# Swapping the order of the recurrent product's blocks between even and odd steps

## The reference

```python
h = silu(cond @ W1.T + b1)
gate = sigmoid(h @ W2.T + b2)
x = x + (x + x * gate)        # x * (2 + gate)
```

```python
def step(prev_h, xw):                   # xw = x[:, t] @ Wx + b
    next_h = tanh(prev_h @ Wh + xw)
    return next_h, next_h
x = x + h_t
```

## Time and profile before

| what | us |
|---|---|
| median of 3 runs (197.01 to 197.09) | 197.02 |
| the profiled execution | 196.62 |
| its span, first to last instruction | 194.8 |
| TensorE matmuls busy | 176.0 |
| TensorE weight loads busy | 167.4 |
| VectorE busy | 98.2 |
| ScalarE busy | 85.3 |

### The profile page before, as it was taken

How to read it: one execution, slowest core, us unless ns; L and a number is a source line. 1 busy time by engine, 2 the same in 40 slices (tenths; PEclk the granted TensorE clock), 3 DMA queues, 4 the chain that set the end, 5 groups by cost and what they waited for, 6 DMA issues and landing times.

```text
span 194.8 us, 33383 instructions
## 1 busy us (share of the span) xinstructions
PE 176.0 (90%) x15962; PEld 167.4 (86%) x15962; DVE 98.2 (50%) x395; ACT 85.3 (44%) x518; POOL 0.5 (0%) x5
## 2 busy tenths in 40 slices
PE   4899999999999999999999999999999999999995
PEld 2698988988898898889889889888988988898895
DVE  0445465455546545555554654555465455545543
ACT  3234444444444444444444444444444444444442
POOL 1000000000000000000000000000000000000000
PEclk9999999999999999999999999999999999999999
DMA  6309999702020020202002020200202020020212
GB/s 200 109 30 320 397 415 406 294 1 108 0 107 3 0 109 0 108 0 107 1 2 108 0 109 0 106 2 2 108 0 108 0 100 9 0 109 0 108 54 54
DMA packets 7105, 17.98 MB, mean 92 GB/s; under 512 B 1459, under 2 KB 2867, under 8 KB 7094
## 3 DMA queue, kind: packets, MB, share of 16 engines
q1 hardware_dynamic: 6656, 17.32, 23.8%
q10 hardware_dynamic: 438, 0.55, 0.8%
HBM read 9.48 MB, written 8.39 MB: 92 GB/s over the span
## 4 chain that ended last, share of the span: by engine, by line
PE 86%; ACT 7%; issue 3%; DMA 3%; SPq 0%
PE bank_e L193 48%; PE bank_l L193 38%; ACT h_ring L178 7%; DMA w_t<-in_w 3%; SPq L129 0%
## 5 line engine op out<-in xcount | busy, mean ns | idle before, releaser
L193 PE MATMUL bank_e<-h_ring,wh_sb 128*32 128x32 f32 x4096 | 98.6, 204 | 13.5 <-ACT h_ring L178 13.5
L178 ACT ACTIVATE h_ring<-bank_e 128x32 f32<-128x32 f32 x256 | 50.5, 197 | 101.7 <-PE bank_e L193 101.7
L193 PE MATMUL bank_l<-h_ring,wh_sb 128*32 128x32 f32 x4096 | 91.2, 196 | 0.0
L193 PEld LDWEIGHTS bank_e<-h_ring,wh_sb 128*32 128x32 f32 x4096 | 71.5, 108 | 20.2 <-ACT h_ring L178 20.1
L193 PE MATMUL bank_l<-x_ring,wx_sb 128*32 128x32 f32 (+1 forms) x4112 | 81.0, 200 | 0.0
L341 DVE TENSOR_TENSOR x<-x,h_ring 128x128 f32<-128x128 f32 x129 | 37.6, 291 | 84.0 <-ACT h_ring L178 84.0
L193 PE MATMUL bank_e<-x_ring,wx_sb 128*32 128x64 f32 (+1 forms) x2056 | 71.0, 224 | 0.0
L193 PEld LDWEIGHTS bank_l<-h_ring,wh_sb 128*32 128x32 f32 x4096 | 69.8, 113 | 0.0
L193 PEld LDWEIGHTS bank_l<-x_ring,wx_sb 128*32 128x32 f32 (+1 forms) x4112 | 64.5, 111 | 0.0
L193 PE MATMUL bank_l<-ones,b_sb 128*32 128x32 bf16 (+1 forms) x1026 | 51.7, 180 | 0.0
L178 ACT ACTIVATE h_ring<-bank_l 128x32 f32<-128x32 f32 x256 | 50.4, 197 | 0.0
(11 more groups left out here) (31 smaller groups left out, 14.0 us busy)
## 6 DMA issues: line engine op xcount, KB each, us to landing
x<-in_x SPq DMA_DIRECT2D x15, 512.0 KB, 9.5
out_dram<-x SPq DMA_DIRECT2D x15, 512.0 KB, 3.5
w_t<-in_w SPq DMA_DIRECT2D x1, 256.0 KB, 5.4
wx_sb<-in_wx SPq DMA_DIRECT2D x1, 256.0 KB, 5.7
wh_sb<-in_wh ACTq DMA_DIRECT2D x1, 256.0 KB, 5.0
x<-in_x SPq DMA_DIRECT2D x1, 256.0 KB, 3.1
out_dram<-x SPq DMA_DIRECT2D x1, 256.0 KB, 2.5
w_t<-in_w_cond ACTq DMA_DIRECT2D x1, 145.0 KB, 3.8
```

The source lines that it names most:

```text
L178: nc.scalar.activation(h_ring[:, m, s * B:(s + 1) * B], z_of(s, m), ACT.Tanh)\
L193: done = nc.tensor.matmul(out[q:q + columns], weights[:, q:q + columns], moving, start=start, stop=stop, skip_group_check=True)
```

## The change

The condition in the list of orders is turned round. Steps 0 and 2 of a turn now make (0, 0), (1, 0), (0, 1), (1, 1), in which half one of z is whole after two blocks; steps 1 and 3 now make (0, 0), (0, 1), (1, 0), (1, 1), in which it is whole after three. The fills, the waits for each half of h and the number of matmuls are the same.

```diff
-                    order = [(0, 0), (1, 0), (0, 1), (1, 1)] if s % 2 else [(0, 0), (0, 1), (1, 0), (1, 1)]
+                    order = [(0, 0), (1, 0), (0, 1), (1, 1)] if s % 2 == 0 else [(0, 0), (0, 1), (1, 0), (1, 1)]
```

## The result

The changed kernel takes 199.26 us (median of 5 runs, 198.83 to 199.62) against 197.01 us before: 1.014 times as long (95% interval 1.012 to 1.017). In a second comparison the same pair came out at 1.017 (1.014 to 1.020), so 3 us is the better figure for the difference. The profiled execution is 199.59 us, 2.97 more than the one before.

What follows compares the result with a forecast made beforehand. The kernel was taken as bound by a loop of latencies, not TensorE's throughput. Late fills add 0.02 x 64 + 0.06 x 63 = 5.1 us to 197.0; with a little regained at the loop's head, 202.0 us, range 200.0 to 205.2.

Steps and rivals of the forecast that it cites:

- The loop of gap + 0.59: Every step, tanh to tanh: a closed loop of latencies, the two tanhs' gap + 0.25 + 0.34 us.
- the exchange of the gaps: Between ScalarE's two tanhs: 0.16 moves to steps 1 and 3, 0.09 to 0 and 2; the turn's sum stays 0.50.
- A: Order (0,0), (1,0), (0,1), (1,1): gap 0.16; the fill after it starts 0.12 us ahead of the tanh, not 0.19.
- the engine was not full: Rival in TensorE: its throughput sets the end, so the time stays 197.0 us; chance 0.06.
- the gap did not jump: Rival at ScalarE's second tanh: gap grows by 0.07 behind late steps, 206.6 us, or 211 if twice a turn; chance 0.08.
- B: Order (0,0), (0,1), (1,0), (1,1): gap 0.09; now in steps 1 and 3, whose fills were to end late.
- Step 1: Its fill ends at +0.32 instead of +0.25, half one's second product 0.03 late: cost 0.02 us a turn, 64 times.
- my low bound: Counting only weight loads: step 1 costs 0.01 or less, step 3 0.045; 0.05 a turn, 3.2 us.
- Step 3: Its fill ends at +0.36, half one's second product 0.065 late: cost 0.055 to 0.06 us a turn, 63 times.
- The loop's head: Rival at step 0's first products: waits in every fourth turn vanish, 0.6 us gained, 196.4 us; chance 0.04.
- the main case: Late fills in steps 1 and 3 make it slower, 200.2 to 205.2 us; chance 0.82.

Runs made afterwards that it cites:

- the shorter fill: Changed kernel with the wide block moved to step 2's fill and 4 bias records moved from step 1's to step 3's fill: 1.001 of the kernel before.
- the extra block: Changed kernel with one block of 8 records added to step 3's fill: 1.051 of the kernel before; same addition in the kernel before: 1.032.
- all B: Changed kernel with the order (0,0), (0,1), (1,0), (1,1) in all four steps: 1.008 of the kernel before.
- the split kernel: Changed kernel with block (0,1) split in two, half before and half after block (1,0), in all steps: 1.017 of the kernel before.

## Why the prediction was too high

**The mechanism held.** The loop of gap + 0.59, the exchange of the gaps, the fills that start 0.07 closer to their tanh behind A, the place of the loss (steps 1 and 3, not 0 and 2) and the order of the two costs all came as written. The wide block moved from step 3's to step 2's fill (2.860) takes step 3's loss away, the shorter fill takes step 1's away, and the extra block adds its whole length. The rivals fell: the engine was not full, and the gap did not jump: it stayed 0.09 behind the late B steps.

**Step 1: 0.02 forecast, 0.017 measured** (0.761 against 0.744). That this agrees is in part luck. TensorE's matmuls in this step, of which the rows are the first of half one's second product and its last:

```profile
98.44 0.21 PE L193 MATMUL bank_e<-h_ring,wh_sb 128*32 128x32 f32 x1
...
98.54 0.20 PE L193 MATMUL bank_e<-h_ring,wh_sb 128*32 128x32 f32 x1
```

The second product started 0.42 after the tanh at 98.02, not 0.45. Its records then took 0.10 where I had 0.065, and the tanh at 98.78 followed the last one by 0.24 instead of 0.26. These errors nearly cancel. The loads alone, my low bound, have it right: 0.42 against 0.41.

**Step 3: 0.06 forecast, 0.041 measured.** This is the step that failed: "I take the middle because the trace shows matmuls 0.03 behind their loads in a full stream". The loads' own reckoning, which I had set down as the low bound, gave the second product of half one at +0.46 against 0.41 and a cost of 0.045; it was loaded at +0.45. Half one's last matmul was indeed recorded as late as I had added up, 0.55 after the tanh (0.48 and 0.065), but the next tanh followed it sooner:

```profile
99.99 0.20 PE L193 MATMUL bank_e<-h_ring,wh_sb 128*32 128x32 f32 x1
100.00 0.20 PE L193 MATMUL bank_l<-h_ring,wh_sb 128*32 128x32 f32 x1
100.00 0.20 PE L193 MATMUL bank_e<-h_ring,wh_sb 128*32 128x32 f32 x1
100.02 0.25 PE L193 MATMUL bank_l<-h_ring,wh_sb 128*32 128x32 f32 x6
```

The last record on bank_e starts at 100.00 and the tanh at 100.24: 0.24. In the kernel before, the last of the eight records from 96.44 starts near 96.51 (their row lasts 0.27, one matmul 0.20), and the tanh comes at 96.77: 0.26. My reading is that after a wait the records start in a burst, while in a full stream they are spread out and stand nearer to the work itself; all B, below, bears it out. From the first load of half one's second product to the tanh it is 0.34 in both. A distance from a recorded matmul start in a waiting step must not be added to a start in a full stream. The Trainium skill has a line that fits (Perfetto Trace Analysis, Summary: the profiler window per engine type): for TensorE the start is that of the operands' prefetch and the end is estimated. The trace agrees in so far as a recorded start is no fixed time ahead of the tanh: 0.24 and 0.26 above.

**The loop's head: up to 0.6 us forecast as a rival's gain, of which I counted 0.1; it came whole.** The stall of every fourth turn made the kernel before 2.851 a turn instead of 2.843. In the changed kernel no steady turn shows it, neither in the tanhs nor in step 0's first load, which comes 0.25 after its tanh in every one: the mean of 2.901 is the sum of the four steps. The 0.008 a turn are 0.5 us. It is no rival to the main case but a term of its own sum, since both rest on TensorE's place against the tanh, and it had a row of its own. The store, which I gave as its cause, is not it (stores moved half a turn, above).

**The sum, then:** 0.017 x 64 + 0.041 x 63 - 0.5 = 3.2 us, where the mean turns give 3.1, the two comparisons 2.8 (1.014) and 3.3 (1.017), and I had 5.0. Of the 1.9 us between 5.0 and the turns' 3.1, step 3 makes 1.2, step 1 0.2 and the loop's head 0.4 beyond the 0.1 counted. The low bound took the two costs nearly right (0.05 a turn, 3.2 us) but only 0.2 off for the loop's head; with the 0.5 it gives 199.7, still above the 199.26 measured. That last part, the 0.8 us between the turns' 3.1 and the 2.3 of the medians, no run explains.

**What my later expectations got wrong.** B behind B was put at 0.705 and is 0.72. Two blocks take 0.12 in recorded loads after a wait (96.13 to 96.25) but 0.13 in a full stream, and the first number is a burst. That error of 0.013 in all four steps turned a forecast gain of 2 us into a loss of 1.5. All B itself shows it, for its step 3 runs in a full stream and lasts 0.72 all the same (tanhs at 98.04 and 98.76). Half one's second product is loaded there at

```profile
98.42 0.11 PEld L193 LDWEIGHTS bank_e<-h_ring,wh_sb 128*32 128x32 f32 x1
```

which is 0.38 after the one tanh and 0.34 ahead of the other, where the steps that wait have 0.36 and 0.35. So the recorded starts shift and the work does not. It is the same mistake as in step 3.

## What to carry to other kernels

When a loop of latencies is the bound, reckon each piece of filler work by when it may start and when it has to end: the order of the blocks that depend on the loop can be neutral for the loop and still shift that window, here by 0.07 us. Before swapping such an order, look which steps carry the longest filler and put the order with the early finish behind them, or move filler to a step with cover; here the same change then cost nothing that could be measured (1.001). Measure distances for such sums between events of the same kind in the same state, both after a wait or both in a full stream, and take an idle stretch for free room only when its idle time is a wait for data, not "issue".

## What the runs showed of the hardware

- Going round TensorE's loop takes 0.37 to 0.42 us from the last weight load of a turn to the next load, even where that waits for nothing (97.93 to 98.33), with 0.045 more in every second, third or fourth turn or in none, depending on the kernel and not on the stores. The Trainium skill gives about 0.11 us for a compare-and-branch (Advanced Engine Details and Errata, Control Flow Timing). No row here shows the branch alone; the whole way round costs three to four times that figure.
- Records of neighbouring blocks on different banks mix by one to three records in a full stream, as the rows from 98.27 and from 99.99 on show.
- ScalarE's second tanh follows the first by 0.09 behind B, where half two's last record starts 0.06 to 0.07 after half one's, by 0.16 behind A and by 0.13 in the split kernel, where it starts about 0.13 after it in both. Why A and B add 0.03 and the split order nothing is open.
- One more block in the loop brought a single stop of 2.07 and 1.86 us in the first turns, in the changed kernel and in the one before.
